# One-core AdaLN, gated scan and mixture of experts: transposes put side by side, routing with fewer small instructions

## The chip, the core and the metric

One core of a Trainium2 chip runs the whole program in one launch. The core has TensorE (PE in the profile, with its weight loads as PEld), VectorE (DVE), ScalarE (ACT), GpSimd (POOL) and SyncE (SP, which here only starts DMAs). The metric is the time of the launch in microseconds (us). Before the change three runs gave 852.9, 852.83 and 851.2 us, median 852.83.

## The reference

The input is x, 2 x 2048 tokens of 256 numbers. The part that the change touches is the routing and the experts; the rest is short here.

```
h  = layernorm(x) * (1 + ca) + sa
# attn part: RMS norm, three 256x256 products, a causal scan, RMS norm ("second norm"), a gated 768-wide FFN
xn = rmsnorm(h);  g, v, d = xn@Wg+bg, xn@Wv+bv, xn@Wd+bd
h  = h + scan(sigmoid(g)*tanh(v), 0.001+0.998*sigmoid(d))
xn = rmsnorm(h);  h = h + (silu(xn@W_gate) * (xn@W_up)) @ W_out
x  = x + ga * h
# experts
h  = layernorm(x) * (1 + cb) + sb                       # h2, the row that is routed
scores = softmax(h @ router_w)                          # 8 experts
expert_weights, expert_idx = top_k(scores, 2)
y_e = (gelu(h @ w1[e]) * (h @ v1[e])) @ w2[e]           # width 704
x  = x + gb * (sum over the two chosen of weight * y_e + bias)
```

## The kernel before

**Products.** Every large product is made at fp32 accuracy from three matmuls: operands are split into a high and a low part and `three` (lines 614 to 616) issues high by high, low by high and high by low. TensorE needs its operands with the contracted dimension on the partitions, so rows are transposed on TensorE first: a group of `pe.transpose` calls with the identity in `cn`, 128 x 128 each. ACT copies the result out of PSUM as the high part, DVE makes the low part.

**Dense part.** The 4096 tokens are 8 blocks of 512. Step r works on several blocks at once, and each engine has its own written order, `step(r)`, for r = 2 to 7, with hand-written lists around it. TensorE does in step r: `gvd` (six products of block r), `xn2_transposes` (second norm of block r-1, two groups of four transposes, c = 0 and 1), `rank_tokens` (block r-4), `h2_transposes` (rows to be routed of block r-3, again two groups of four), `gate_up` (twelve products, r-1), `router_logits` (r-3), `ffn_out` (r-2), `state_transposes` and `xn_transposes` (eight transposes each). A group of four or eight transposes writes one or two of the PSUM banks `tp[0]` and `tp[1]`; `wait_transpose` makes it wait until the last reader of that bank is done.

**Routing.** For each block DVE runs `choose` (the two largest of eight logits per token, and a one-hot `hot` for each), `count` (how many tokens chose each expert so far, `seen_b`), `slots` (the row in DRAM to which each token goes) and `weigh` (the gate weights). Between them TensorE runs `rank_tokens`: the rank of each token among those that chose the same expert is a prefix sum, made by 128 x 128 bf16 matmuls with a triangle and with ones, 14 matmuls of 8 columns for a block (lines 724, 726, 727). Then POOL scatters the rows of the block to the DRAM tensor `routed` by eight indirect DMAs (`scatter`, line 2009). `chain` and `link` make each small DVE instruction wait for the one before.

**Experts.** 71 tiles of 128 routed rows follow. The first five (`EARLY`) belong to one expert, picked when five blocks are counted, and run between the last dense products; `picked_expert` loads its number from SBUF into a register of the engine (line 507). All later tiles take expert and row from a table, which is ready when all blocks are counted. In `tile_step(t)` TensorE does: `hid_transposes(t-1)` (six transposes, line 777), `first_products(t)` (18 matmuls), `x_transposes(t+1)` (two transposes, line 743), `second_product(t-1)` (17 matmuls). ACT does `gelu(t)`, `xT_split(t+1)`, `hidT_split(t)`. DVE does `multiply(t)` (lines 1645 and 1646), `xT_rest(t+1)` (1636), `gate_y(t-1)`, `hidT_rest(t)`, `take_gates(t+1)`. SP loads the rows of a tile (`x_moe`, four buffers) when the tile four before has let go of its buffer. `x_transposes(t+1)` waits for the rows and for `xT_l`, the count that `xT_rest(t)` raises, since both use one PSUM bank; `first_products(t)` waits for the same count. Tiles 5 to 10 and 67 to 70 are written out; the rest is a loop with four tiles a turn.

**Fillers.** `fill` issues matmuls of ones whose results nobody reads, in places where TensorE would wait between the dense part and the expert tiles.

## Time and profile before

| | before |
|---|---|
| time, median of 3 runs | 852.83 us (851.2 to 852.9) |
| profiled execution: its own time | 847.11 us |
| its span, first to last instruction | 845.3 us |
| mean granted TensorE clock | 0.993 |
| PE busy | 824.0 us, 97% |
| DVE busy | 559.4 us, 66% |
| ACT busy | 376.7 us, 45% |
| POOL busy | 489.3 us, 58% |

How to read it: the profile is of one execution, which was 5.7 us shorter than the median of the timed runs. Three stages follow each other: the dense steps up to about 290 us, a mixed stretch from 290 to 391 us in which the last dense products, the routing of the last blocks and the first five expert tiles are interleaved, and the expert tiles from 391 to 832 us. Matmuls overlap in the records: the time that one costs its engine is the distance from its start to the next start, not its length. A granted clock of 1.00 is 2.4 GHz, and 0.50 is 1.2 GHz. The profile shows 0.50 for about 3.4 us at 342 us and again at 386 us, and from 840 us to the end.

### The profile page before, as it was taken

Reading aid. Unit: us, or ns where it says so; the run is one execution under the profiler, and the core shown is the slowest. Engines: PE = TensorE matmul, PEld = TensorE weight load, DVE = VectorE, ACT = ScalarE, POOL = GpSimd, SP = SyncE. Lnnn points to the kernel's source line nnn. Section 1 sums busy time; section 2 is a strip of 40 time slices with the busy share of each in tenths; the row PEclk is TensorE's granted clock in tenths of the full one; section 3 lists DMA queues with packets and bytes.
Section 4 is the critical chain, followed back from the end, with each engine's and each line's share of the span. In section 5 each row is a group of like instructions: output and inputs, shape, how many; then the busy total and the mean of one; then the engine's idle time right before and its main releaser. Section 6 shows DMA issues by size and latency. Waiting matters only on the chain.

```text
span 845.3 us, 18996 instructions
## 1 busy us (share of the span) xinstructions
PE 824.0 (97%) x5078; PEld 726.9 (86%) x5079; DVE 559.4 (66%) x1555; ACT 376.7 (45%) x681; POOL 489.3 (58%) x454
## 2 busy tenths in 40 slices
PE   8899999999999999998999999999999999999995
PEld 4678898989888888878999999999999999999994
DVE  6788768878775849886556556555655555555553
ACT  5884656575665525444234234224233242342321
POOL 2353645868685886579645646447537465383332
PEclk9999999999999999999999999999999999999998
DMA  8131050303020261427522422524324322222221
GB/s 268 51 110 50 2 181 23 105 26 102 7 96 18 84 224 49 158 91 197 150 47 39 139 44 36 150 44 116 65 38 138 51 36 44 38 37 38 38 44 27
DMA packets 49984, 67.65 MB, mean 80 GB/s; under 512 B 4944, under 2 KB 44240, under 8 KB 49936
## 3 DMA queue, kind: packets, MB, share of 16 engines
q1 hardware_dynamic: 36272, 47.71, 18.1%
q0 software_dynamic: 13664, 19.35, 12.1%
q8 instruction: 24, 0.39, 0.2%
q14 instruction: 24, 0.20, 0.1%
HBM read 43.51 MB, written 23.54 MB: 79 GB/s over the span
## 4 chain that ended last, share of the span: by engine, by line
PE 84%; DVE 5%; POOL 4%; issue 2%; ACT 1%; DMA 1%; DVEq 0%; SPq 0%; ACTq 0%; POOLq 0%
PE ps L614 24%; PE ps L615 23%; PE ps L616 23%; PE ps L777 6%; POOL routed L2009 2%; PE ps L743 2%; PE ps L715 1%; PE ps L820 1%; PE ps L819 1%; PE ps L632 1%; PE ps L660 1%; PE ps L702 1%; PE ps L667 1%; DVE sg_sb L1499 1%; POOL hid_lo L1970 0%
## 5 line engine op out<-in xcount | busy, mean ns | idle before, releaser
L614 PE MATMUL ps<-split,xT_moe_hi 128*128 (+2 forms) x426 | 167.0, 392 | 0.1
L615 PE MATMUL ps<-split,xT_moe_lo 128*128 (+2 forms) x426 | 160.7, 377 | 0.0
L616 PE MATMUL ps<-split,xT_moe_hi 128*128 (+2 forms) x426 | 160.4, 377 | 0.0
L2021 POOL TENSOR_TENSOR y_moe<-y_moe 128x256 f32<-128x256 f32 x69 | 66.0, 956 | 124.4 <-DVE y_moe L1654 124.4
L2031 POOL DMA_INDIRECT out_rows<-y_moe,tok_moe x71 | 111.1, 1565 | 28.7 <-issue 21.4
L1176 ACT ACTIVATE hidT_hi<-ps 128x768 fp32r<-128x768 f32 x70 | 56.9, 812 | 150.4 <-PE ps L777 150.4
L1170 ACT ACTIVATE gelu_moe<-ps 128x704 f32<-128x704 f32 x71 | 53.9, 759 | 124.6 <-PE ps L616 124.5
L614 PE MATMUL ps<-split,hidT_hi 128*128 (+1 forms) x355 | 105.9, 298 | 0.5 <-DVE hidT_lo L1696 0.5
L616 PE MATMUL ps<-split,hidT_hi 128*128 (+1 forms) x355 | 100.1, 282 | 0.0
L615 PE MATMUL ps<-split,hidT_lo 128*128 (+1 forms) x355 | 100.0, 282 | 0.0
L1654 DVE SCALAR_TENSOR_TENSOR y_moe<-ps,gate_moe,gates 128x256 f32<-128x256 f32 x138 | 60.4, 479 | 53.5 <-PE ps L820 53.3
L1970 POOL TENSOR_TENSOR hid_lo<-hf_sb,hid_hi 128x512 fp32r<-128x512 f32 x48 | 67.9, 1415 | 43.3 <-ACT hid_hi L1148 43.1
L614 PEld LDWEIGHTS ps<-split,xT_moe_hi 128*128 128x128 f32 x426 | 80.9, 190 | 12.8
L615 PEld LDWEIGHTS ps<-split,xT_moe_lo 128*128 128x128 f32 x426 | 80.9, 190 | 12.5
L616 PEld LDWEIGHTS ps<-split,xT_moe_hi 128*128 128x128 f32 x426 | 80.5, 189 | 12.8
L1661 DVE TENSOR_TENSOR hidT_lo<-ps,hidT_hi 128x640 fp32r<-128x640 f32 x70 | 57.7, 824 | 39.0 <-ACT hidT_hi L1176 39.0
L2009 POOL DMA_INDIRECT routed<-rows,slot_i x64 | 69.8, 1091 | 18.7 <-issue 18.7
L614 PE MATMUL ps<-xn2T_hi,gu_hi 128*128 128x512 f32 x192 | 77.2, 402 | 0.2 <-DVE xn2T_lo L1516 0.2
L616 PE MATMUL ps<-xn2T_lo,gu_hi 128*128 128x512 f32 x192 | 75.0, 390 | 0.0
L615 PE MATMUL ps<-xn2T_hi,gu_lo 128*128 128x512 f32 x192 | 75.0, 390 | 0.0
L404 POOL TENSOR_TENSOR split<-raw,split (+2 forms) x21 | 72.9, 3858 | 0.0
L1645 DVE TENSOR_TENSOR hid_moe<-ps,gelu_moe 128x64 f32<-128x64 f32 x71 | 16.0, 225 | 84.9 <-ACT gelu_moe L1170 66.5
(231 smaller groups left out, 2017.0 us busy)
## 6 DMA issues: line engine op xcount, KB each, us to landing
raw<-in_w SPq DMA_DIRECT2D x9, 1408.0 KB
x_moe<-routed SPq DMA_DIRECT2D x74, 132.5 KB, 2.3
raw<-in_w SPq DMA_DIRECT2D x9, 640.0 KB
x_again<-in_x SPq DMA_DIRECT2D x8, 512.0 KB, 4.5
out_rows<-x_again SPq DMA_DIRECT2D x8, 512.0 KB, 3.0
x_sb<-in_x SPq DMA_DIRECT2D x7, 512.0 KB, 3.5
gu_raw<-in_gu_t SPq DMA_DIRECT2D x1, 1536.0 KB, 9.0
raw<-in_w SPq DMA_DIRECT2D x18, 64.0 KB
```

Of the source, the lines that this page charges most:

```text
L404: i = eng.tensor_tensor(w_moe_lo(e, o, size), raw[:, bass.ds((e & 1) * RAW_SLOT + o, size)], f32(w_moe_hi(e, o, size)), ALU.subtract)
L614: pe.matmul(dst, a_hi, b_hi, start=first, stop=False)
L615: pe.matmul(dst, a_lo, b_hi, start=False, stop=False)
L616: return pe.matmul(dst, a_hi, b_lo, start=False, stop=last)
L1170: act.activation(gelu_moe[:], a_ps, ACT.Gelu).then_inc(gelu_r, 1)
L1176: act.activation(hidT_hi[:].rearrange("p k n -> p (k n)"), hidT_ps(t), ACT.Copy).then_inc(hidT_h, 1)
L1654: i = v.scalar_tensor_tensor(y_moe[:, t.slot, b, :], y_of(t), gate_moe[:, t.slot, 3 - b:4 - b], gates[:, b, 1, :], ALU.mult, ALU.mult)
L1661: v.tensor_tensor(hidT_lo[:].rearrange("p k n -> p (k n)"), hidT_ps(t)[:, 0:full], f32(hidT_hi[:, 0:KF - 1, :].rearrange("p k n -> p (k n) ...
L1970: g.tensor_tensor(hid_lo[:, m, :], hf_sb[:, m % 2, :], f32(hid_hi[:, m, :]), ALU.subtract).then_inc(hid_l, 1)
L2009: g.indirect_dma_start(routed, bass.IndirectOffsetOnAxis(ap=slot_i[:, q % 2, k, i:i + 1], axis=0), rows[:, q % 2, i, :], None)\
L2021: g.tensor_tensor(y_moe[:, t.slot, 0, :], y_moe[:, t.slot, 0, :], y_moe[:, t.slot, 1, :], ALU.add)\
L2031: g.indirect_dma_start(out, bass.IndirectOffsetOnAxis(ap=tok_moe[:, t.slot, :], axis=0), y_moe[:, t.slot, 0, :], None, compute_op=ALU.add) ...
```

## The change

TensorE: `rank_tokens` takes 5 matmuls a block in place of 14. One has 32 columns (all four groups of 128 tokens by the triangle), three have 24, 16 and 8 columns (ones by the groups before), and one has 32 columns, with `seen_b` read four times over. In the dense step both groups of `xn2_transposes` stand behind `gvd(r, 1)`, and both of `h2_transposes` ahead of `gate_up(r-1, 0)`. In the expert tiles above `EARLY` the two transposes of the next tile stand right behind the six of the tile before, ahead of `first_products`. DVE: `hot` and `pos_k` are made by one instruction of 64 elements each in place of two of 32; `take_gates` of the early tiles leaves out the multiplication by one, and the picked expert's number is loaded once, ahead of `choose(5)`, and kept.

```diff
@@ rank_tokens
-                for i in range(TPB):
-                    pe.matmul(ranks[:, i, :], tri[:], chosen_b[:, i, :], start=True, stop=False)
-                    for j in range(i):
-                        pe.matmul(ranks[:, i, :], ones[:], chosen_b[:, j, :], start=False, stop=False)
-                    mm = pe.matmul(ranks[:, i, :], ones[:], seen_b[:, q % 2, :], start=False, stop=True)
-                mm.then_inc(rank_mm, 1)
+                pe.matmul(ranks[:], tri[:], chosen_b[:], start=True, stop=False)
+                for j in range(1, TPB):
+                    pe.matmul(ranks[:, j:TPB, :], ones[:], chosen_b[:, 0:TPB - j, :], start=False, stop=False)
+                pe.matmul(ranks[:], ones[:], seen_b[:, q % 2, :].unsqueeze(1).to_broadcast([P, TPB, E]),
+                          start=False, stop=True).then_inc(rank_mm, 1)
@@ tensor: tile_step
                 hid_transposes(t.near(-1))
+                if t.n > EARLY and not final(t):
+                    x_transposes(t.near(1))
                 first_products(t, e)
-                if not final(t):
+                if t.n == EARLY:
                     x_transposes(t.near(1))
@@ tensor: step
                     gvd(r, 0)
-                if on(r - 1):
-                    xn2_transposes(r - 1, 0)
                 if on(r):
                     gvd(r, 1)
                 if on(r - 1):
+                    xn2_transposes(r - 1, 0)
                     xn2_transposes(r - 1, 1)
@@
                     h2_transposes(r - 3, 0)
+                    h2_transposes(r - 3, 1)
                 if on(r - 1):
                     gate_up(r - 1, 0)
-                if on(r - 3):
-                    h2_transposes(r - 3, 1)
-                if on(r - 1):
                     gate_up(r - 1, 1)
@@ choose
-                for k in range(2):
-                    a = v.tensor_tensor(hot[:, k], iota, top_f[:, :, k:k + 1].to_broadcast([P, TPB, E]), ALU.is_equal)
-                link(a)
+                link(v.tensor_tensor(hot[:], iota.unsqueeze(1).to_broadcast([P, 2, TPB, E]),
+                                     top_f[:].rearrange("p i k -> p k i").unsqueeze(3).to_broadcast([P, 2, TPB, E]), ALU.is_equal))
@@ slots
-                for k in range(2):
-                    i = v.tensor_tensor(pos_k[:, k], pos[:], hot[:, k], ALU.mult)
-                link(i)
+                link(v.tensor_tensor(pos_k[:], pos[:].unsqueeze(1).to_broadcast([P, 2, TPB, E]), hot[:], ALU.mult))
@@ take_gates
+                if early(t):
+                    gate = x_moe[:, t.slot, bass.ds(e + D, 1)]
+                    v.wait_ge(rows_in[t.slot], t.round * 16 + 16)
+                else:
...
+                v.tensor_scalar(g[:, 2:3], tok, float(S), gate, ALU.is_ge, ALU.mult)
+                v.tensor_scalar(g[:, 3:4], tok, float(S), gate, ALU.is_lt, ALU.mult)
@@ vector, between the dense part and the tiles
             hidden(7, 5)
+            expert = picked_expert(v)
             choose(5)
             split_lo(v, PICKED, 2)
             slots(5)
-            take_gates(Tile(0))
+            take_gates(Tile(0), expert)
```

The order of TensorE at the turn of an expert tile, before (hidT is the transposed hidden row of the tile before, xT that of the tile itself, 777 are the six transposes of the hidden rows):

```order
L820 MATMUL ps<-split,hidT_hi 128x256
L499 TENSOR_LOAD tab
L499 ISA x2
L777 MATMUL ps<-cn,hid_moe 128x128 x6
L750 REGISTER_ALU
L614 REGISTER_ALU
L614 ISA
L614 MATMUL ps<-split,xT_moe_hi 128x512
```

and in the changed kernel, where lines 776 and 742 are the old 777 and 743:

```order
L819 MATMUL ps<-split,hidT_hi 128x256
L499 TENSOR_LOAD tab
L499 ISA x2
L776 MATMUL ps<-cn,hid_moe 128x128 x6
L742 MATMUL ps<-cn,x_moe 128x128 x2
L749 REGISTER_ALU
L614 REGISTER_ALU
L614 ISA
L614 MATMUL ps<-split,xT_moe_hi 128x512
```

The pair of transposes of the next tile has moved up past the 18 matmuls of `first_products`; it stood behind them, ahead of the products on hidT.

The order of TensorE in the first dense step that ranks a block, before (667 is `xn2_transposes`):

```order
L667 MATMUL ps<-cn,xn_sb 128x128 x4
L724 MATMUL ps<-chosen_b,tri 128x8
L727 MATMUL ps<-seen_b,ones 128x8
L724 MATMUL ps<-chosen_b,tri 128x8
L726 MATMUL ps<-chosen_b,ones 128x8
L727 MATMUL ps<-seen_b,ones 128x8
L724 MATMUL ps<-chosen_b,tri 128x8
L726 MATMUL ps<-chosen_b,ones 128x8 x2
L727 MATMUL ps<-seen_b,ones 128x8
L724 MATMUL ps<-chosen_b,tri 128x8
L726 MATMUL ps<-chosen_b,ones 128x8 x3
L727 MATMUL ps<-seen_b,ones 128x8
```

and in the changed kernel:

```order
L667 MATMUL ps<-cn,xn_sb 128x128 x8
L723 MATMUL ps<-chosen_b,tri 128x32
L725 MATMUL ps<-chosen_b,ones 128x24
L725 MATMUL ps<-chosen_b,ones 128x16
L725 MATMUL ps<-chosen_b,ones 128x8
L726 MATMUL ps<-seen_b,ones 128x32
```

Fourteen small matmuls are five, and the first four transposes, which stood six matmuls further up, have joined the second four.

The order of DVE from the last instruction of `slots(5)` through `take_gates` of tile 0, before:

```order
L1615 CAST slot_i<-slot_f 128x8
L507 TENSOR_LOAD pick_i
L507 ISA x2
L1625 ISA
L1625 TENSOR_SCALAR gate_moe<-x_moe,ones_f 128x1
L1628 TENSOR_SCALAR gate_moe<-x_moe,gate_moe 128x1
L1629 TENSOR_SCALAR gate_moe<-x_moe,gate_moe 128x1
L1632 CAST tok_moe<-x_moe 128x1
```

and in the changed kernel:

```order
L1610 CAST slot_i<-slot_f 128x8
L1627 ISA
L1627 TENSOR_SCALAR gate_moe<-x_moe 128x1
L1628 TENSOR_SCALAR gate_moe<-x_moe 128x1
L1631 CAST tok_moe<-x_moe 128x1
```

The load of the expert's number (507) has gone from here to a place ahead of `choose(5)`, and one instruction on the gate is gone.

## Rows read from the trace of the kernel before

**Rows 1.** The page: busy time of the engines; the chain's shares by engine.

```profile
PE 824.0 (97%) x5078; PEld 726.9 (86%) x5079; DVE 559.4 (66%) x1555; ACT 376.7 (45%) x681; POOL 489.3 (58%) x454
...
PE 84%; DVE 5%; POOL 4%; issue 2%; ACT 1%; DMA 1%; DVEq 0%; SPq 0%; ACTq 0%; POOLq 0%
```

**Rows 2.** Busy time by stretch: window, its us, engines' busy us, PEclk, DMA, GB/s.

```profile
55.00:290.00 235.00, 235.00 (x1421) 206.16 (x1420) 177.31 (x463) 141.34 (x315) 156.19 (x141) 1.00 0.18 63
391.00:832.00 441.00, 441.00 (x2821) 404.26 (x2820) 259.69 (x721) 154.94 (x217) 235.66 (x220) 1.00 0.33 72
386.00:390.00 4.00, 3.91 (x14) 3.32 (x15) 2.92 (x12) 0.81 (x1) 4.00 (x3) 0.57 0.59 97
```

**Rows 3.** Timeline, PE, ranks of a block: start us, length us, instruction.

```profile
140.49 0.17 PE L724 MATMUL ps<-chosen_b,tri 128*128 128x8 bf16 x1
...
140.84 0.47 PE L614 MATMUL ps<-xnT_hi,gvd_hi 128*128 128x512 f32 x1
141.16 0.39 PE L615 MATMUL ps<-xnT_hi,gvd_lo 128*128 128x512 f32 x1
141.39 0.40 PE L616 MATMUL ps<-xnT_lo,gvd_hi 128*128 128x512 f32 x1
```

**Rows 4.** The chain's pieces, groups of transposes: start us, us, what.

```profile
164.77 0.87 PE ps L660 x8
...
502.35 0.65 PE ps L777 x6
...
506.80 0.22 PE ps L743 x2
...
509.04 0.65 PE ps L777 x6
```

**Rows 5.** Timeline, PE, the products behind the two transposes.

```profile
506.78 0.36 PE L614 MATMUL ps<-split,hidT_hi 128*128 x1
506.98 0.28 PE L615 MATMUL ps<-split,hidT_lo 128*128 x1
507.10 0.28 PE L616 MATMUL ps<-split,hidT_hi 128*128 x1
```

**Rows 6.** Timeline, DVE, low part of the next tile's rows.

```profile
507.83 0.41 DVE L1636 TENSOR_TENSOR xT_moe_lo<-ps,xT_moe_hi 128x256 fp32r<-128x256 f32 x1
```

**Rows 7.** Timeline, PE, the turn to the next tile.

```profile
508.87 0.82 PE L777 MATMUL ps<-cn,hid_moe 128*128 128x128 f32 x6
509.45 0.48 PE L614 MATMUL ps<-split,xT_moe_hi 128*128 x1
```

**Rows 8.** The page, DMA issues: rows of a tile, KB each, us to landing.

```profile
x_moe<-routed SPq DMA_DIRECT2D x74, 132.5 KB, 2.3
```

**Rows 9.** Timeline, second norm's low part on DVE, and gate_up's start on PE.

```profile
142.07 0.69 DVE L1516 TENSOR_TENSOR xn2T_lo<-ps,xn2T_hi 128x512 fp32r<-128x512 f32 x1 [1.62 <-ACT xn2T_hi L1136]
...
145.40 0.48 PE L614 MATMUL ps<-xn2T_hi,gu_hi 128*128 128x512 f32 x1
```

**Rows 10.** Timeline, PE, the wait behind the ranks of block 4.

```profile
295.47 1.23 PE L702 MATMUL ps<-cn,rows 128*128 128x128 f32 x8 [0.54 <-DVE xn2T_lo L1516]
```

**Rows 11.** Timeline, DVE, take_gates of tiles 0 and 1, and what follows.

```profile
333.11 0.21 DVE L1625 TENSOR_SCALAR gate_moe<-x_moe,ones_f 128x1 f32 x1 [0.87 <-issue]
...
335.81 1.67 DVE L1556 SCALAR_TENSOR_TENSOR rows<-rows,rstd,mod 128x256 f32<-128x256 f32 x4
```

**Rows 12.** Timeline, PE, the transposes that wait for those rows.

```profile
337.54 0.66 PE L702 MATMUL ps<-cn,rows 128*128 128x128 f32 x4 [0.23 <-DVE rows L1556]
```

**Rows 13.** Timeline, DVE, routing of block 7.

```profile
363.06 0.29 DVE L1576 TENSOR_TENSOR hot<-cn,top_f 128x32 f32<-128x32 f32 x2
...
366.52 0.22 DVE L1612 TENSOR_REDUCE slot_f<-pos_k 128x8 f32<-128x64 f32 x1
```

**Rows 14.** The chain from the scatters of block 7 to tile 5.

```profile
368.66 0.99 POOL routed L2009
...
384.90 0.44 PE ps L743 x2
```

More of the change, by code:

```diff
@@ L1615, in slots, with take_gates @@
                 v.tensor_copy(slot_i[:, q % 2], slot_f[:]).then_inc(slots_r, 1)
-            def take_gates(t):
-                e = picked_expert(v) if early(t) else entry(v, TAB_EXPERT, t, E - 1)
-                keep = ones_f[:, 0:1] if early(t) else mask[:, bass.ds(t.column, 1)]
+            def take_gates(t, e=None):
                 g, tok = gate_moe[:, t.slot, :], x_moe[:, t.slot, D + E:D + E + 1]
-                v.wait_ge(rows_in[t.slot], t.round * 16 + 16)
-                if t.n == EARLY:
-                    v.wait_ge(mask_r, 1)
-                v.tensor_scalar(g[:, 0:1], x_moe[:, t.slot, bass.ds(e + D, 1)], keep, None, ALU.mult)\
-                    .then_inc(gate_steps, 1)
-                v.wait_ge(gate_steps, t.v + 1)
-                v.tensor_scalar(g[:, 2:3], tok, float(S), g[:, 0:1], ALU.is_ge, ALU.mult)
-                v.tensor_scalar(g[:, 3:4], tok, float(S), g[:, 0:1], ALU.is_lt, ALU.mult)
+                if early(t):
+                    gate = x_moe[:, t.slot, bass.ds(e + D, 1)]
+                    v.wait_ge(rows_in[t.slot], t.round * 16 + 16)
+                else:
+                    e = entry(v, TAB_EXPERT, t, E - 1)
+                    gate = g[:, 0:1]
+                    v.wait_ge(rows_in[t.slot], t.round * 16 + 16)
+                    if t.n == EARLY:
+                        v.wait_ge(mask_r, 1)
+                    v.tensor_scalar(gate, x_moe[:, t.slot, bass.ds(e + D, 1)], mask[:, bass.ds(t.column, 1)], None, ALU.mult)\
+                        .then_inc(gate_steps, 1)
+                    v.wait_ge(gate_steps, t.v + 1 - EARLY)
+                v.tensor_scalar(g[:, 2:3], tok, float(S), gate, ALU.is_ge, ALU.mult)
+                v.tensor_scalar(g[:, 3:4], tok, float(S), gate, ALU.is_lt, ALU.mult)
                 if t.n >= SLOTS:
@@ L1886, in _ @@
             slots(5)
-            take_gates(Tile(0))
+            take_gates(Tile(0), expert)
             weigh(5)
             add_ffn(7, 0)
-            take_gates(Tile(1))
+            take_gates(Tile(1), expert)
             norm2_scale(6)
@@ L1912, in _ @@
             xT_rest(Tile(3))
-            take_gates(Tile(2))
+            take_gates(Tile(2), expert)
             slots(7)
@@ L1928, in _ @@
             xT_rest(Tile(5))
-            take_gates(Tile(3))
+            take_gates(Tile(3), expert)
             gate_y(Tile(3))
-            take_gates(Tile(4))
+            take_gates(Tile(4), expert)
             hidT_rest(Tile(4))
```

## The prediction

> **What bounds the kernel now.** I read the page first. PE is busy for 824 of 845.3 us, and 84% of the chain that ended last is PE [rows 1]. So the question for each edit is whether it shortens PE's own queue, or a wait of PE. The table by stretch says where PE waits: not at all in the dense steps (235.00 of 235 us busy) and not at all in the expert tiles (441.00 of 441 us) [rows 2]. There a shorter PE queue is gained in full and a faster VectorE is worth nothing. Only between 290 and 391 us does PE wait, and there a gain on PE can be lost in a wait and a gain on VectorE can be worth something. The timelines and the chain give the prices.
>
> **Ranks: 9 matmuls fewer for each of 8 blocks.** Fourteen matmuls start between 140.49 and 140.84 us, so one costs 0.35 / 14 = 0.025 us [rows 3]. They are of 8 columns; the new ones have 8 to 32, which no row shows. Streaming bounds them: a matmul of 512 columns costs 0.23 us (141.16 to 141.39, [rows 3]), so 32 columns stream in 0.014 us, below the 0.025 that each pays anyway. From below the price of the large ones is 0.025, from above 0.025 + 0.014 = 0.039. I take 0.025, since streaming overlaps between neighbours in these rows. A block then saves 9 x 0.025 = 0.225 us (with the upper price for four of the five 0.17). Eight blocks are 1.8 us, if nothing takes it back. The Trainium skill, page "TensorE: Matmul & The Clock Gate", section "Wait — 56ns, not 53.3ns?", puts the start-to-start distance at about 25 ns also for 32 columns at full clock; by it the sum would use the lower price, as mine does.
>
> **Joined transposes in the expert tiles, 64 times, and 11 times in the dense steps.** The number of transposes is the same; a gain exists only if each group pays something for being a group. The chain shows groups of three sizes: 2 cost 0.22 us, 6 cost 0.65, 8 cost 0.87 [rows 4]. That is 0.11 each at every size, with no fixed part: 0.22 + 0.65 = 0.87, just what one group of eight costs in this same program. So the edit that touches most of the run is worth 0.00 us a tile. The resolution of these rows is 0.01 us, so the bounds are -0.01 and +0.01 us a tile, 0.6 us either way over 64 tiles. I take 0.2 us of gain. There is one row that speaks against it: the first product behind the two transposes holds PE for 0.20 us (506.78 to 506.98) and the next one for 0.12 [rows 5]. The 0.08 looks like a switching cost. I do not count it as one, because neighbouring records overlap and this product starts inside the record of the last transpose; counted over the whole group, from the product ahead to the product behind, the pair takes its 0.22 us and no more [rows 4]. This reading is the first rival.
>
> **What the moved transposes wait for.** In a tile the pair now needs the rows of the next tile and the count `xT_l` about 3.8 us (18 products) sooner. Rows land 2.3 us after their issue [rows 8], and they are issued three tiles ahead of use, some 20 us at 6.7 us a tile; four us sooner leaves them in time. `xT_l` is raised by the instruction that ends at 507.83 + 0.41 = 508.24, and the new place of the pair is behind the six transposes that start at 508.87, at the place where the first product now starts, 509.45 [rows 6, 7]: a slack of 1.2 us. It shrinks by 0.22 us, because the first products and with them `multiply` come later by the pair's own time. ScalarE and VectorE gain a little room behind it, since they split the next tile's rows without waiting for the pair. Nothing is gained or lost there.
>
> **Moved transposes in the dense steps.** The first group for the second norm comes one product group later (1.4 us, six products of 0.23), and ScalarE, which works in order, does the copy, a copy of hidden values and an activation later by up to that. The low part on VectorE ends at 142.07 + 0.69 = 142.76, `gate_up` starts at 145.40 [rows 9]. 2.6 us of slack take a delay of 1.4 us. The groups for the routed rows come together ahead of `gate_up`; the second waits for the bank that `gate_up` waits for as well. Cost 0, down to -0.01 us a group.
>
> **What reaches the end, block by block.** Ranks of blocks 0 to 3 stand in the dense steps, where PE never waits: 4 x 0.225 = 0.90 us, all of it gained, as the other engines there follow PE.
> Block 4: behind its ranks, fillers and then 0.54 us of wait for VectorE's low part [rows 10]. PE arrives sooner and waits longer: 0.
> Block 5: its 0.225 us are followed by a wait of 0.23 us for `rows` from VectorE [rows 12]. PE arriving sooner would lengthen this wait, but here VectorE's trims count. In `take_gates` of tile 0 VectorE stands idle for 0.87 us behind the load of the expert's number, and the instruction that goes took 0.21; the same instruction goes for tile 1, straight ahead of the four that write `rows` (335.81) [rows 11]. That is some 1.2 us less ahead of them, so the wait ends with PE's own arrival: 0.225 + 0.23 = 0.46 us. The load itself now stands ahead of `choose(5)`, beside the last hidden product of VectorE, where it may cost 0.1 us that later stalls cover.
> Block 6: 0.225 us, PE is on the chain up to the copies of block 7: gained.
> Block 7: its routing is on the chain, through ranks and slots to the eight scatters and the load of tile 5, which PE meets at 384.90 [rows 14]. Two instructions of 32 elements take 0.29 us together, one that reads 64 takes 0.22 [rows 13]. For `hot` and for `pos_k` that is 0.07 each, with the ranks' 0.225 together 0.365 us. The scatters and the load are not touched.
> The trims of VectorE in all other blocks lie beside a busy PE: 0.
>
> Sum: 0.90 + 0 + 0.46 + 0.225 + 0.365 = 1.95 us, and 0.2 for the joined groups, 2.15 us. Against the profiled execution of 847.1 us that gives 845.0 (span 843.2). The timed median is 5.7 us above that execution, at no place that the rows name, so I take the same difference from the median: 852.8 - 2.2 = 850.6 us.
>
> **The rivals.**
> 1. *A group of transposes does pay for being one.* For: the 0.08 us behind the pair [rows 5]. Then 64 tiles save 64 x 0.08 = 5.1 us, the dense steps 11 x 0.08 = 0.9, with my sum (less the 0.2) 7.9 us: 844.9. Against: sizes 2, 6 and 8 on one line through zero [rows 4]. A part of it, 0.03 us a tile, would give 848.6.
> 2. *Little of it reaches the end.* The gains are a fifth of a us each and the stretch from 290 to 391 us has its own pace: eight scatters in a row on POOL and a load [rows 14]. If blocks 5 to 7 lose theirs in it, the 0.9 us of blocks 0 to 3 remain: 851.9. For: two of the four late ranks have a wait right behind them [rows 10, 12]. Against: what ends these waits is downstream of PE or of the trimmed VectorE.
> 3. *The pair stalls the tiles.* PE takes its instructions in order, and behind the pair are 18 products and all that follows. It decides when `xT_l` and what the sequencer does behind it take longer than the 1.2 - 0.2 = 1.0 us of slack. If they miss by 0.1 us a tile, the cost is 64 x 0.1 = 6.4 us less the 2 us gained: 857.2. For: the new wait stands at each of 64 tiles. Against: `first_products` waits for the same count today at the same place and PE was never idle for it [rows 2].
> 4. *The clock.* PE runs at 2.4 GHz in the tiles (granted 1.00), and at half of it in part of 386 to 390 us (0.57 in that window) [rows 2]. The gained time lies in the mixed stretch too, so one stretch at 1.2 GHz more or less may come of any shift. The lost time is half of its length; (1 - 0.57) x 4 us = 1.7 us. This widens the range and has no sign. The Trainium skill, same page, section "Part 4: PE-mode transpose", says that transposes do not count as PE work for the clock gate, which would speak against putting eight in a row. In this trace six in a row, 0.65 us, stand in every tile and the grant stays 1.00; eight are 0.87 us of 6.7, the same share of a tile as before.
>
> **How the numbers follow.** Forecast (ranks and block 5 to 7 as summed) 0.58; rival 1, whole or in part, 0.12; rival 2 0.22; rival 3 0.08. 0.2% of the time, 1.7 us, is about what a measurement of this kernel can tell from no change. The forecast is just beyond it: with the clock and the spread of the runs (851.2 to 852.9) some four fifths of its chance, 0.47, fall under 851.1, and 0.11 between. Faster 0.47 + 0.12 = 0.59; the same 0.11 + 0.22 = 0.33; slower 0.08. Range: from the forecast down by one stretch of clock and a part of rival 1, 848.0, up to rival 2 with some spread, 852.8.
>
> **What would show it.** In the profile after: five rank matmuls within some 0.13 us where 0.35 stood; PE still at 100% in both long stages. A tile's length is the test for the joined groups: 6.69 us as now (502.35 to 509.04, [rows 4]) means that they are worth nothing; 6.61 would mean rival 1, 6.8 or an idle time ahead of line 742 rival 3. PE's meeting with tile 5 should come near 384.9 - 1.95 = 383.0 us; if it comes at 384.0, rival 2 is right. The 0.23 us wait for `rows` should be gone and the 0.87 us idle on VectorE too. I am wrong if the dense steps (55 to 290 us) do not end some 0.9 us sooner, or if the tiles alone shorten by more than 1 us.

## The result: 4.1 us faster where 2.2 were forecast

| | before | after |
|---|---|---|
| median of 6 runs beside each other, us | 851.62 (851.09 to 852.90) | 847.53 (846.98 to 848.89) |
| ratio, 95% interval | | 0.9944 [0.9932, 0.9956] |
| the profiled execution, its span | 847.11, 845.3 | 848.34, 846.2 |

The change is faster by 3.7 to 5.8 us; forecast were 2.2 us and 848.0 us as the lowest time. Of the 3.1 us between 850.6 and 847.5 us, 1.2 lie in the starting point: the forecast subtracts from the median of three runs, 852.8, and six runs have 851.6. The rest, 1.9 us, is the gain itself. The two profiled spans give the wrong sign: the execution profiled before took 847.1 us, below all six timed ones beside it, and by its time belongs to the faster sets of the last section. So I first read the stretches, not the span.

The page of the kernel after, busy time and the chain's shares, as [rows 1]:

```profile
PE 818.6 (97%) x5006; PEld 724.6 (86%) x5007; DVE 557.7 (66%) x1534; ACT 367.9 (43%) x681; POOL 485.8 (57%) x454
...
PE 87%; POOL 3%; DVE 3%; issue 1%; ACT 1%; DMA 1%; another core or an unknown queue 0%; ACTq 0%; DVEq 0%; POOLq 0%
```

72 matmuls of ranks fewer (8 x 9) and the same picture: PE is the chain. Busy time by stretch (window, its us, engines, granted clock, DMA), as [rows 2]:

```profile
55.00:290.00 235.00, 235.00 (x1391) 206.80 (x1390) 180.83 (x458) 141.49 (x319) 155.65 (x143) 1.00 0.19 62
391.00:832.00 441.00, 439.96 (x2815) 405.36 (x2814) 259.64 (x720) 147.40 (x217) 236.37 (x222) 1.00 0.34 72
```

The columns behind the engines are the granted clock, the DMA share and GB/s. PE still never waits in the dense steps. In the tiles it now waits for 1.03 us in one place, and that is new: the forecast had looked for 100% there. The timeline of PE at the ranks, as [rows 3]: start, length, instruction, and at the end the count of instructions in the row:

```profile
140.52 0.18 PE L723 MATMUL ps<-chosen_b,tri 128*128 128x32 bf16 x1
140.54 0.22 PE L725 MATMUL ps<-chosen_b,ones 128*128 128x24 bf16 x3
140.62 0.18 PE L726 MATMUL ps<-seen_b,ones 128*128 128x32 bf16 x1
140.65 0.48 PE L614 MATMUL ps<-xnT_hi,gvd_hi 128*128 128x512 f32 x1
```

Five matmuls in 140.65 - 140.52 = 0.13 us, 0.026 each, where 0.35 stood: the lower price was the right one. The chain's pieces at the joined transposes of a tile, as [rows 4]:

```profile
496.53 0.66 PE ps L776 x6
497.19 0.22 PE ps L742 x2
...
503.22 0.66 PE ps L776 x6
503.88 0.22 PE ps L742 x2
```

Eight cost 0.88, and a tile 503.22 - 496.53 = 6.69 us, as before: rival 1 is not there in the tiles. Rival 3 neither, since nothing stands idle ahead of line 742. On VectorE the routing of block 7, as [rows 13], and the gates of tiles 0 and 1 with what follows, as [rows 11]:

```profile
361.37 0.22 DVE L1573 TENSOR_TENSOR hot<-cn,top_f 128x64 f32<-128x64 f32 x1
...
367.50 0.22 DVE L1606 TENSOR_TENSOR pos_k<-pos,hot 128x64 f32<-128x64 f32 x1
```

```profile
332.26 0.21 DVE L1627 TENSOR_SCALAR gate_moe<-x_moe 128x1 f32<-128x1 f32 x1
...
334.37 1.67 DVE L1554 SCALAR_TENSOR_TENSOR rows<-rows,rstd,mod 128x256 f32<-128x256 f32 x4
```

0.22 for the joined instruction as priced, and no idle time ahead of the gates. PE's transposes for block 6 start with no wait (337.10 us, against 337.54 behind 0.23 of wait in [rows 12]). The waits of PE in the mixed stretch after are these (waits of PE from 290 to 410 us: us in total, times, longest):

```profile
PE ps L776 <- DVE hid_moe L1645: 2.2, 2, 1.2
...
PE ps L837 <- DVE slot_i L1610: 0.7, 1, 0.7
...
PE ps L702 <- DVE xn2T_lo L1514: 0.2, 1, 0.2
```

The wait of [rows 10] went from 0.54 to 0.2, where the forecast had it growing. At the early count (line 837), the matmul behind the fillers that waits for the slots of block 4, PE waits 0.7 us for `slot_i`; before it was 0.25, and the forecast did not name this wait. PE meets tile 5 at 386.15 us in this profile, where 383.0 was the sign of the forecast. In the fourth run of the whole (e14), which is free of the losses of the last section, it is 348.47 us from the first state transposes to that meeting, against 351.29 us before: 2.8 us less, where 1.95 was forecast.

### The profile page after: what moved, and what is told of

The parts are those of the page before. It is cut to its first block, busy times and chain, and to the rows that moved or that the text cites. A ratio compares the mean times of both kernels' runs of the same rounds, so it can differ in the third digit from the quotient of the medians.

```text
span 846.2 us, 18804 instructions
## 1 busy us (share of the span) xinstructions
PE 818.6 (97%) x5006; PEld 724.6 (86%) x5007; DVE 557.7 (66%) x1534; ACT 367.9 (43%) x681; POOL 485.8 (57%) x454
## 4 chain that ended last, share of the span: by engine, by line
PE 87%; POOL 3%; DVE 3%; issue 1%; ACT 1%; DMA 1%; another core or an unknown queue 0%; ACTq 0%; DVEq 0%; POOLq 0%
PE ps L614 24%; PE ps L616 24%; PE ps L615 24%; PE ps L776 5%; PE ps L742 2%; PE ps L715 1%; POOL routed L2009 1%; DMA out_rows<-y_moe,tok_moe 1%; PE ps L819 1%; PE ps L818 1%; PE ps L660 1%; PE ps L702 1%; PE ps L632 1%; PE ps L667 1%; POOL out_rows L2031 1%
## 5 line engine op out<-in xcount | busy, mean ns | idle before, releaser
L614 PE MATMUL ps<-split,hidT_hi 128*128 (+1 forms) x355 | 99.9, 281 | 1.3 <-DVE y_moe L1653 0.7
L616 PE MATMUL ps<-split,hidT_hi 128*128 (+1 forms) x355 | 99.9, 281 | 0.0
```

The costliest lines, as they stand in the source:

```text
L614: pe.matmul(dst, a_hi, b_hi, start=first, stop=False)
L616: return pe.matmul(dst, a_hi, b_lo, start=False, stop=last)
```

## Experiments

Sixteen kernels ran, each five rounds beside the kernel before, and each set of four on one chip. Every profile is one execution, but the lengths of the stretches between fixed points on PE repeat to 0.04 us between profiles where PE does not wait. So the stretches carry the shares of the parts, and the timed ratios the size of the whole.

### Each part alone, beside 848.22 us

The ranks alone:

```
-for i in range(TPB): tri; ones for each j < i; ones with seen_b
+pe.matmul(ranks[:], tri[:], chosen_b[:], ...) and the rest of the five
```

> The kernel before with the five rank matmuls a block in place of fourteen, and nothing else changed. The measured gain of the whole change is 4.1 us, twice my sum. My theory of the sum: this part gives 1.35 to 1.8 us (0.225 us a block, some of it lost behind block 4), so 849.8 to 850.3 against 851.6. Rival, the missing 2 us sit in the mixed stretch from 290 to 391 us, in waits that fall out one way or another by small shifts: then any part that shifts the stretch by some tenths of a us can show 2 us more or less than its own sum, and this one shows more than 2.5 us or less than 0.7. In the profile a block's ranks take some 0.13 us and the dense steps end 0.9 us sooner in both cases.

Measured 847.52, 0.9995 [0.9985, 1.0004]. The transposes of a tile alone:

```
 hid_transposes(t.near(-1))
+if t.n > EARLY and not final(t): x_transposes(t.near(1))
 first_products(t, e)
```

> The kernel before with the pair of x transposes joined to the six hidden ones in the 64 expert tiles above the early ones, nothing else. My theory: 0.00 to 0.01 us a tile, 0.2 us in all, so 851.4 against 851.6 and a tile of 6.69 us in the profile. Rival 1 of the prediction (a group pays for being a group): 0.03 to 0.08 us a tile, 2 to 5 us, 846.5 to 849.6, which would be the missing half. Rival 3: the wait of tile 7 for hidden rows (1.0 us) that the profile of the changed kernel shows comes from this edit, then it is here too.

Measured 847.32, 0.9992 [0.9982, 1.0001]. The transposes of the dense steps alone:

```
-xn2_transposes(r - 1, 0)
 gvd(r, 1)
+xn2_transposes(r - 1, 0)
 xn2_transposes(r - 1, 1)
```

> The kernel before with both groups of the second norm and both of the routed rows joined in the dense steps, nothing else. My theory: eleven joins worth 0.00 to 0.01 us, so 851.6 and no verdict. Rival: ScalarE takes its copies in another order of time and the dense steps hand over to the mixed stretch in another phase; then PE busy stays 235.00 of 235 us in the dense steps and the time still moves by over 1 us, through the stretch from 290 to 391 us.

Measured 847.28, 0.9985 [0.9976, 0.9994]. VectorE's edits alone:

```
-for k in range(2): v.tensor_tensor(hot[:, k], ...)
+v.tensor_tensor(hot[:], ...)            (pos_k likewise)
-e = picked_expert(v)                    (in take_gates)
+expert = picked_expert(v)               (once, ahead of choose(5))
```

> The kernel before with the edits on VectorE alone: hot and pos_k by one instruction each, one instruction fewer in take_gates of the early tiles, and the picked expert's number loaded once. My theory: 0.23 us (the wait of PE for rows of block 6) and 0.14 us for block 7, so 851.2. Rival: the mixed stretch is paced by VectorE and POOL in the timed runs, and the 0.87 us of idle time behind the load of the number comes back in full and more: 1.5 to 3 us, 848.6 to 850.1, which would be the missing half.

Measured 846.69, 0.9978 [0.9968, 0.9989]. What follows: alone they are worth 0.05, 0.08, 0.15 and 0.22%, together 0.50% or 4.2 us. The intervals of the first two hold no change as well, so only the last two are clear of it. The largest is the one that the forecast valued at 0.37 us, and the smallest is the one it put first.

### The whole again, the kernel before again, and all but one part, beside 847.68 us

The whole, and the kernel before, unchanged:

> The changed kernel itself, a second time, beside the kernel before. Between the first two comparisons the kernel before itself moved from 851.6 to 848.2 us, and each of the four parts alone gave 0.05 to 0.22%, 4.2 us together against 848.2. Theory A, the parts add up: 0.9950 of the kernel before, as in the first comparison (0.9944), whatever that takes today. Theory B, the 4.1 us of the first comparison hold a part that belongs to the chip or the hour (the kernel before lost 3.4 us there that the changed one did not): then the ratio is 0.9965 to 0.998, which is my sum of 2.15 us give or take 0.6.

> The kernel before, unchanged, as if it were a change: how far a comparison of a kernel with itself comes from 1, and a second profile of it. Both theories expect a ratio of 1.000 within 0.001. Theory B expects that its own waits between 290 and 391 us differ from those of the first profile by 1 us or more in some place.

Measured 843.24, 0.9938 [0.9925, 0.9951], and 847.67, 0.9998 [0.9989, 1.0006]. The whole without the edits on VectorE, and without the joined ranks:

```
-hot, pos_k in one instruction, one load of the expert's number, gates without the product by ones
```

> The changed kernel without its edits on VectorE: ranks and joined transposes alone. Theory A (parts add up, VectorE's is the largest with 0.22%): 0.9972 of the kernel before. My sum: the wait for rows of block 6 and 0.14 us of block 7 come back, so 0.4 us over the whole change. Rival: without VectorE's trims the ranks' gain in blocks 4 to 7 is only wait on PE, as in the profile of the ranks alone (0.69 us of wait behind the ranks of block 6), and the ratio is over 0.998.

```
-ranks in five matmuls
```

> The changed kernel with the fourteen rank matmuls a block as before. My sum gives the ranks 1.55 of 2.15 us, so this kernel should lose most of the gain: ratio 0.9993. Theory A with the measured parts gives the ranks 0.05% alone, and then this kernel stays at 0.995 to 0.996 of the kernel before. In between: ranks worth 0.9 us, all of it in the dense steps, 0.996 to 0.997.

Measured 846.36, 0.9980 [0.9970, 0.9989], and 845.52, 0.9970 [0.9960, 0.9981]. The ranks are worth 0.32% on top of the rest where alone they were 0.05%; VectorE's edits 0.42% where alone they were 0.22%. As times these differences are weak: each hangs on the one ratio of the whole in this set, the lowest of its four, and has an interval of some 0.17% either way; with the mean of the four, 0.9950, the ranks on top are worth 0.20%. The profiles show that the parts lean on each other. With the ranks alone (e1) the dense steps are 0.81 us shorter, but only 0.39 of it is left at the early count, where PE waits 0.68 us for the slots; with VectorE's edits beside them (e15, below) 0.85 is left.

### Which of VectorE's edits, beside 851.68 us

```
-link(v.tensor_tensor(hot[:], ...))
+for k in range(2): a = v.tensor_tensor(hot[:, k], ...)        (pos_k likewise)
```

> The whole change, but hot and pos_k are written by two instructions each again; take_gates and the load of the expert's number stay changed. Leaving all VectorE edits out cost 0.42% less 0.0x: the whole stood at 0.9938, without them at 0.9980. Theory A (the idle load of the expert's number carries it, because it stands ahead of `rows`, for which PE waits, and the small instructions are 0.07 us a block): this kernel stays near the whole, ratio 0.9940 to 0.9950. Theory B (the routing chain of blocks 5 to 7 is what PE waits for everywhere from 290 to 391 us, and each 0.14 us of it counts three or four times): at least half of the 0.42% is lost, ratio 0.9960 or more.

```
-def take_gates(t, e=None):
+def take_gates(t):
+    e = picked_expert(v) if early(t) else entry(v, TAB_EXPERT, t, E - 1)
```

> The whole change, but take_gates and its load of the expert's number as before; hot and pos_k stay joined. Theory A: most of the 0.42% is lost, ratio 0.9965 to 0.9980, and in the profile the wait of PE for `rows` of block 6 (line 702, 0.2 us) and the idle 0.9 us on VectorE in front of take_gates of tile 0 are back. Theory B: at most half of it, ratio 0.9940 to 0.9960.

Measured 848.81, 0.9964 [0.9951, 0.9976], and 848.71, 0.9971 [0.9961, 0.9981]; the whole beside them had 0.9966, so the times tell nothing. The timelines do. The profile of e9 fell on its slowest run (853.2 us, the other five 847.5 to 849.5), so I read it only up to the early count, 264.52 us behind its first state transposes. PE there:

```profile
299.70 0.18 PE L837 MATMUL ps<-seen_b,ones 128*128 128x8 bf16 x1 [1.22 <-DVE slot_i L1613]
```

The whole waits 0.73 there (e14, below). Two joined instructions take 0.49 us out of this wait; their own lengths, 0.29 less 0.22 each, explain 0.14. VectorE and GpSimd ahead of it tell the rest: start, length, instruction, first VectorE and then GpSimd of e9,

```profile
295.56 3.62 DVE L1608 TENSOR_TENSOR pos_k<-pos,hot 128x32 f32<-128x32 f32 x2
299.21 0.22 DVE L1610 TENSOR_REDUCE slot_f<-pos_k 128x8 f32<-128x64 f32 x1
299.47 0.17 DVE L1613 CAST slot_i<-slot_f 128x8 int32<-128x8 f32 x1
```

```profile
294.29 2.51 POOL L1973 TENSOR_TENSOR hid_lo<-hf_sb,hid_hi 128x512 fp32r<-128x512 f32 x2 [2.42 <-ACT hid_hi L1146]
296.76 2.36 POOL L1993 TENSOR_TENSOR x_again<-x_again,mod 128x1024 f32<-128x1024 f32 x1
```

and the same of the whole (e14):

```profile
295.30 1.32 DVE L1606 TENSOR_TENSOR pos_k<-pos,hot 128x64 f32<-128x64 f32 x1
296.66 0.22 DVE L1607 TENSOR_REDUCE slot_f<-pos_k 128x8 f32<-128x64 f32 x1
296.91 1.98 DVE L1610 CAST slot_i<-slot_f 128x8 int32<-128x8 f32 x1
```

```profile
294.03 2.51 POOL L1970 TENSOR_TENSOR hid_lo<-hf_sb,hid_hi 128x512 fp32r<-128x512 f32 x2 [2.84 <-ACT hid_hi L1146]
296.50 2.36 POOL L1990 TENSOR_TENSOR x_again<-x_again,mod 128x1024 f32<-128x1024 f32 x1
```

An instruction of 0.17 us takes 1.98, and it ends at 298.89, just behind the end of GpSimd's `x_again` at 298.86. In e9 the second `pos_k` ends at 299.18, just behind 299.12. (The instruction ahead is held in the same way, by `hid_lo`, to 296.62 in the whole.) In all 18 profiles every `pos_k` and `slot_i` that takes over 0.5 us here ends 0.03 to 0.09 us behind an instruction of GpSimd. So GpSimd's instruction holds these small instructions of VectorE until its end, and what counts is how many of them are still to come when it ends: `slot_f` and `slot_i` in e9, none in the whole. `slot_f`, a reduction, runs beside `x_again` in its usual 0.22. The Trainium skill, page "SBUF — State Buffer", section "SBUF: two separate sides", says that VectorE and GpSimd share a pair of ports under an exclusive lock, held for a whole instruction, and that VectorE's instructions with two inputs in SBUF or in a two-port mode need it; the rows of `pos_k` (two inputs) and `slot_f` (one) fit that, and whether the cast `slot_i` runs in such a mode no row shows.

The forecast had this block at 0, beside a busy PE. Taking the gates' edit out (e10) leaves the 0.73 at 0.72, but brings back the idle time ahead of the gates on VectorE:

```profile
332.01 0.21 DVE L1620 TENSOR_SCALAR gate_moe<-x_moe,ones_f 128x1 f32 x1 [0.86 <-issue]
```

and the stretch from the logits of block 5 to the transposes of block 6 is 14.09 us where every kernel with the edit and joined ranks has 13.62 or 13.63: 0.46 us. So A is right for block 6. At the early count one instruction more costs several times its length, as B says, but at the slots of block 4, where B had not looked. PE's wait for `rows`, which A expected back, is back with 0.30 us.

### The whole a third and fourth time, before a third time, ranks with VectorE

```
 the whole change, unchanged
```

> The whole change once more, beside the three others on the same chip. Ratio to before 0.9938 to 0.9945 again. Its profile shows which of the one-off losses return: the wait of PE at tile 6 of 1.0 to 1.3 us (in both profiles so far) and the stretches at half clock near 342, 359 and 385 us (none near 385 in both profiles so far, one in each profile of every kernel without the whole change).

Measured 849.41 beside 851.68, 0.9966 [0.9954, 0.9977].

> The kernel before, with a profile of its own beside those of the whole change. The whole profiled on two chips (medians of before 851.6 and 851.7 us there) shows PE losing 1.2 to 1.6 us at 308 us, in the load of the expert's weights, and 1.5 us more between the scatters of block 7 and the meeting with tile 5; on the chips where before takes 848 us neither is there. If these two belong to the chip and not to the change, the profile of before shows both where before is timed at 851 to 852 us, and none where it is timed at 848. If they belong to the change, before shows neither at either time, and the gain is understated by 3 us on such a chip.

> The whole change once more. Its three ratios so far are 0.9944, 0.9938 and 0.9966, which spread wider than any one of their intervals; the prediction's 2.2 us is 0.9975. If the middle of the three holds, 0.9945 to 0.9955 (3.8 to 4.7 us); 0.9965 or more would mean that the prediction missed by less than the first measurement said.

Measured 847.67, 0.9997 [0.9989, 1.0006], and 844.03, 0.9954 [0.9941, 0.9967], beside 847.82. The four ratios of the whole, 0.9944, 0.9938, 0.9966 and 0.9954, have a mean of 0.9950, 4.2 us; they spread from 2.9 to 5.3 us, wider than one interval says. The forecast's 2.2 us are below all four. The profile of e14 has neither of the two losses, near 308 us and before tile 5, that the expectation of e13 names; the last section has more on them.

```
 ranks in five matmuls, VectorE's edits; no transposes joined
```

> The joined ranks and the VectorE edits, no transposes joined anywhere. The sum of the parts measured alone is 0.05% + 0.22%, 2.3 us, ratio 0.9973. If ranks need VectorE's trims to reach the end (on top of the others they were worth 0.32%), ratio 0.9950 to 0.9960, most of the whole change. In the profile the dense steps are 0.8 us shorter than before (0.27 a block), the wait of PE for `rows` of block 6 is gone, and the tiles take 410.75 us from tile 8 to 69 as before.

Measured 844.69, 0.9964 [0.9952, 0.9975]. The profiles of these three, PE at the first state transposes and at the early count: the kernel before, ranks with VectorE, the whole.

```profile
33.49 1.09 PE L660 MATMUL ps<-cn,sg_sb 128*128 128x128 f32 x8
...
295.36 1.23 PE L702 MATMUL ps<-cn,rows 128*128 128x128 f32 x8 [0.53 <-DVE xn2T_lo L1516]
...
299.11 0.18 PE L836 MATMUL ps<-seen_b,ones 128*128 128x8 bf16 x1 [0.24 <-DVE slot_i L1615]
```

```profile
33.75 1.09 PE L660 MATMUL ps<-cn,sg_sb 128*128 128x128 f32 x8
...
294.82 1.23 PE L702 MATMUL ps<-cn,rows 128*128 128x128 f32 x8 [0.75 <-DVE xn2T_lo L1515]
...
298.52 0.18 PE L835 MATMUL ps<-seen_b,ones 128*128 128x8 bf16 x1 [0.20 <-DVE slot_i L1611]
```

```profile
34.91 1.09 PE L660 MATMUL ps<-cn,sg_sb 128*128 128x128 f32 x8
...
294.54 0.60 PE L702 MATMUL ps<-cn,rows 128*128 128x128 f32 x4
295.31 0.63 PE L702 MATMUL ps<-cn,rows 128*128 128x128 f32 x4 [0.18 <-DVE xn2T_lo L1514]
...
298.95 0.18 PE L837 MATMUL ps<-seen_b,ones 128*128 128x8 bf16 x1 [0.73 <-DVE slot_i L1610]
```

From the first row to the last it is 265.62, 264.77 and 264.04 us. Without joined transposes PE comes 0.22 us earlier to the wait for `xn2T_lo` and waits 0.22 longer (0.75 for 0.53), just as the forecast said of block 4. With them that wait shrinks to 0.18 and the one for the slots grows from 0.20 to 0.73; this stretch gives 0.73 us more than ranks and VectorE alone.

### A version that beats both

In three of the four profiles of the whole PE waits at tile 6, 0.80 to 1.31 us. (In the fourth, e14, the granted clock is 0.72 from 384 to 390 us, PE comes there 1.5 us later than in e5, and does not wait.) Timelines of e5, PE and then VectorE:

```profile
399.28 0.88 PE L776 MATMUL ps<-cn,hid_moe 128*128 128x128 f32 x6 [1.31 <-DVE hid_moe L1645]
```

```profile
398.01 0.15 DVE L1631 CAST tok_moe<-x_moe 128x1 int32<-128x1 f32 x1 [3.52 <-DMA out_rows<-y_moe,tok_moe]
...
398.34 0.88 DVE L1645 TENSOR_TENSOR hid_moe<-ps,gelu_moe 128x704 f32<-128x704 f32 x1
```

VectorE stands for 3.52 us in `take_gates` of tile 6, until the rows of tile 2 have been added to the output, and `multiply` of tile 6, for which PE waits, is behind it. The further edit:

```
 gate_y(t.near(-1))
+if t.n == EARLY + 1:
+    take_gates(t)
 hidT_rest(t)
...
-take_gates(t.near(1))
+if t.n != EARLY:
+    take_gates(t.near(1))
```

> The whole change and a further edit: VectorE takes the gates of tile 6 one tile later, behind gate_y of tile 5, so that the wait for the rows added by tile 2 (3.5 us on VectorE at 394 us in the profiles of the whole change) no longer stands ahead of multiply of tile 6, for which PE waits 1.0 to 1.3 us. If the profiles of the whole change are typical, that wait is gone from PE and the time is 1.0 to 1.3 us below the whole run beside it (0.12 to 0.15%). Rival: in most executions the wait is hidden or only moves on (the adds on GpSimd are 2.8 us apart, with 10 us of splitting behind the fifth), and the time equals the whole's within 0.1%. Slower than the whole would mean that hidT_rest of tile 6 waits instead.

> The whole change with the gates of tile 6 taken behind gate_y of tile 5. In its first run it was 0.9954 beside 0.9966 for the whole, and PE's wait at tile 6 (1.0 us) was gone from the profile. If that is what it is worth, it is 1.0 us (0.12%) below the whole again; rival: within 0.05% of it, and the difference was spread.

Measured 847.74, 0.9954 [0.9941, 0.9966], beside 0.9966 for the whole; and 841.75, 0.9934 [0.9921, 0.9947], beside 0.9954. That is 1.7 and 2.3 us below the whole, twice with the same sign, and 6.1 us below the kernel before. The intervals of each pair overlap, but in the second set all five runs lie below all five of the whole (841.29 to 843.40 against 843.43 to 845.01). In the profile of the second PE starts tile 6 at 395.77 us with no wait. From tile 5 to tile 8 the two runs take 28.30 and 28.42 us, the whole 29.2 to 29.8 in its four profiles, the kernel before 29.67 to 29.84. That is 0.8 to 1.5 us, as expected; what the times show beyond it is not accounted for.

## Where the gain came from, and where the forecast failed

Lengths on PE in the kernel before (e13) and the whole (e14), same chip:

| from, to | forecast gain | before | whole | gain |
|---|---|---|---|---|
| first state transposes, early count | 0.90 | 265.62 | 264.04 | 1.58 |
| early count, logits of block 5 | 0 | 24.06 | 24.08 | -0.02 |
| to the transposes of block 6 | 0.46 | 14.23 | 13.62 | 0.61 |
| to the logits of block 7 | 0.225 | 21.09 | 20.81 | 0.28 |
| to the meeting with tile 5 | 0.365 | 26.98 | 25.92 | 1.06 |
| tiles 5 to 8 | 0 | 29.80 | 29.81 | -0.01 |
| tiles 8 to 70 | 0.2 | 417.22 | 416.83 | 0.39 |
| the end | 0 | 13.61 | 13.22 | 0.39 |
| sum | 2.15 | 812.60 | 808.32 | 4.28 |

*The price of the joined transposes in the dense steps failed.* The forecast: ranks of blocks 0 to 3, 0.90, and of the moved transposes "Cost 0, down to -0.01 us a group". Ranks and VectorE give 0.85 there, so the ranks were nearly right (0.78 of it in four blocks, 0.20 a block: from the first to the last of the dense steps' state transposes it is 247.41 us for 248.19). The joins give 0.73 on top: the dense steps themselves are 0.54 us shorter (246.87 for 247.41 us), 0.05 us for each of eleven groups; of the 0.57 us that go from the wait behind block 4, 0.53 come back in the wait for the slots, and the remaining 0.19 us lie between the dense steps and the early count. Even in e3, which joins only these, the dense steps are 0.33 us shorter, 0.03 a group. The groups of routed rows show it, from the first transposes to the router's logits (line 715), first in the kernel before (e13), then in e3:

```profile
184.00 0.60 PE L702 MATMUL ps<-cn,rows 128*128 128x128 f32 x4
185.84 0.60 PE L702 MATMUL ps<-cn,rows 128*128 128x128 f32 x4
187.67 1.85 PE L715 MATMUL ps<-rw_sb,hT_sb 128*128 128x8 f32 x16
```

```profile
184.21 1.03 PE L702 MATMUL ps<-cn,rows 128*128 128x128 f32 x8
187.83 1.85 PE L715 MATMUL ps<-rw_sb,hT_sb 128*128 128x8 f32 x16
```

The same eight transposes and twelve matmuls take 3.67 us in two groups and 3.62 joined. The starts tell where it goes: from the first of four transposes to the next matmul it is 0.35 us, less than 4 x 0.11, but that matmul then holds PE for 0.31 to 0.32 in place of 0.23. The forecast set the 0.08 us of rival 1 aside as an overlap of records; the short group covers most of it, but not all. "Sizes 2, 6 and 8 on one line" is the length of the groups alone and says nothing of the matmul behind them. In a tile what is left is 0.006 us, in the dense steps 0.03 to 0.06: a part of rival 1 is true there. Most of the difference between e3's 0.33 and the 0.54, and between 0.20 and 0.225 for the ranks of a block, lies in the 18 matmuls of `gvd` behind the ranks, which take 4.19 to 4.20 us in the kernel before and in the whole, and 4.22 in e3 and e15; why, the runs do not show.

*The trims of VectorE failed too*, in the sentence "The trims of VectorE in all other blocks lie beside a busy PE: 0", and with it the sentence that the 0.90 us of the ranks are "all of it gained". At the early count PE waits for the slots of block 4, and 0.49 us hang on the two joined instructions (e9 against the whole); without joined transposes it is 0.45 (e1 against e15). The price of 0.07 came from the lengths of 0.29 and 0.22, where GpSimd holds nothing up. At the early count a second `pos_k` can get caught by `x_again`. Of the eight profiles with two instructions it is caught in five, e1, e3, e7, e9 and e6, and goes free in the two others of the kernel before and in e2. Since e6 is the kernel before, unchanged, this is not the work of the joined transposes alone: hundredths of a us decide it, and one kernel has it both ways (266.02 us to the early count in e6, 265.62 in e13). The joined `pos_k` is caught by `x_again` in none of the ten profiles that have it. So against e13 the trims prevent a loss, and against e6, where the whole's gain in this stretch would be 1.98 us and not 1.58, they take one away. How often each comes in the timed runs is not shown. I had not looked at who waits behind the fillers of the early count, nor at what GpSimd does beside it.

*Blocks 5 and 6* came as reasoned: the wait for `rows` is gone, 0.61 for 0.46; 0.28 for 0.225.

*Block 7*: of the 1.06 us some 0.7 are no gain of the change. The first profile of before has 26.24 in this stretch, e13 and e6 have 26.98; at 359 us the granted clock is below 1.00 in those two alone of the three. Against 26.24 the gain is 0.32, and 0.365 was forecast. In the same way the end varies from 13.2 to 13.7 us in all kernels. Taking 26.24 and leaving out the end gives 3.2 us as the gain that the stretches account for, 1.0 more than the forecast; 0.68 of that lie in the first stretch, that is in the two steps above.

*The clock.* The forecast gave rival 4 no sign. Windows of 341 to 345 us and 384 to 390 us, in before (e13), ranks with VectorE (e15) and the whole (e14):

```profile
341.00:345.00 4.00, 4.00 (x24) 3.53 (x24) 3.42 (x16) 0.81 (x1) 3.67 (x3) 0.77 0.99 373
384.00:390.00 6.00, 3.94 (x15) 3.08 (x16) 2.73 (x12) 1.20 (x2) 5.77 (x6) 0.79 0.63 107
```

```profile
341.00:345.00 4.00, 4.00 (x23) 3.49 (x22) 3.85 (x18) 1.38 (x2) 3.51 (x4) 1.00 0.86 321
384.00:390.00 6.00, 6.00 (x29) 5.15 (x28) 3.21 (x12) 1.38 (x3) 5.54 (x7) 0.76 0.85 199
```

```profile
341.00:345.00 4.00, 4.00 (x17) 3.48 (x17) 3.46 (x17) 0.81 (x1) 3.81 (x3) 0.57 0.95 355
384.00:390.00 6.00, 5.44 (x21) 4.51 (x22) 3.72 (x15) 1.26 (x3) 5.74 (x5) 0.72 0.68 154
```

At 342 us some executions of a kernel run part of the products at 1.2 GHz and some at 2.4. What that costs depends on VectorE. From the transposes of block 6 to the logits of block 7 (leaving out the chips of the last section) the kernels with VectorE as before take 20.87 to 21.12 us with the half-clock stretch and 20.62 to 20.65 without (e1, e2, e3): PE then waits 0.36 and 0.69 us for VectorE in e1, and most of the time won is lost. With VectorE trimmed it is 20.8 to 21.0 with the half-clock stretch and 19.3 to 19.4 without (e8, e15, e16). So beside the half-clock stretch the trims go with 0.3 us at most in this stretch, and with the full clock at 342 us with 1.2 to 1.4 us. At 385 us the whole shows the opposite: e5 has the clock at 1.00 from 384 to 390 us, gets to tile 6 1.5 us sooner, and waits 1.31 us there. This explains why two profiles of one kernel differ by 1 us and more, and it can be why the timed gain, 3.8 us in this set, is above the 3.2 of the stretches. How often each case comes in the timed runs the runs do not say, so the split of that rest stays open.

*The tiles*: 0.39 us over 62 tiles, 0.006 a tile, inside the 0.00 to 0.01 of the forecast. Rivals 1 (in the tiles) and 3 are refuted by this, rival 2 by the four ratios of the whole. Eight transposes in a row leave the granted clock at 1.00 from 391 to 832 us; the rule of the Trainium skill ("TensorE: Matmul & The Clock Gate", section "Part 4: PE-mode transpose") had spoken against them, and no run shows a loss by it here.

## What to carry to other kernels

Price a small instruction of VectorE by the wait it stands in front of, and look at what GpSimd runs beside it: here one instruction fewer was worth 0.07 us by its length and, with `hot`, 0.49 where GpSimd's 2.36 us caught the one that was left. A cost read at one place of the program (a group of transposes in a tile) holds for that place; read it again where else the edit is made. And parts that shorten two engines which wait for each other are to be summed only together: of 0.81 us that the ranks alone saved PE, 0.39 were left at the next wait for VectorE, and 0.85 with VectorE trimmed.

## What the runs showed beside that

Sets differ by nearly as much as the change. The kernel before took 847.7 to 848.2 us in three sets and 851.6 and 851.7 in the two others. Each set of experiments ran on a chip of its own, so chip and hour are not told apart here; I call it the chip. In the profiles of the latter sets, all of the changed kernel or nearly so, PE stands still near 309 us for nothing that the profile shows, while expert weights are loaded, and VectorE at the slots of block 7; e12:

```profile
309.47 0.40 PE L615 MATMUL ps<-xn2T_hi,gu_lo 128*128 128x512 f32 x1
310.55 0.39 PE L616 MATMUL ps<-xn2T_lo,gu_hi 128*128 128x512 f32 x1 [0.68 <-issue]
```

```profile
369.65 0.19 DVE L1605 TENSOR_TENSOR pos<-ps,cn 128x32 f32<-128x32 f32 x1 [3.37 <-remote]
```

From the early count to the logits of block 5 these profiles have 25.0 to 25.7 us, all others 24.1; to tile 5 28.3 to 29.2 against 25.9 to 27.0. Together that is about 3.5 us, the difference between the medians of before. The whole on a chip of the first kind (e5, e14) shows neither, so it is not the change alone. That before loses the same on such a chip was not shown, as none of its profiles fell on one.

By its time, 847.1 us, and its rows, which show neither loss, the profile that the forecast was made from is of the first kind, and the median that it subtracts from is of the second.
